# Inverse square roots of the last phase's layer norms: from a power on GpSimd to an integer estimate and Newton steps on VectorE

## Chip, cores and metric

The kernel runs on one core of a Trainium2 chip. The metric is the device time of one execution in microseconds. Activations, weights and matmuls are fp32. The engines are named PE (TensorE), DVE (VectorE), ACT (ScalarE), POOL (GpSimd) and SP (SyncE, which issues most DMAs).

## What is computed

64 graphs of 128 nodes with 128 features each ("64 tiles") go through four layers; in each, a graph network and then an expert network are added to x, both behind a layer norm:

```
def _layernorm(x, axis=-1, eps=1e-05):
    m = jnp.mean(x, axis=axis, keepdims=True)
    v = jnp.var(x, axis=axis, keepdims=True)
    return (x - m) / jnp.sqrt(v + eps)
...
x = x + _L0_gnn_ref(_layernorm(x), adj, ...)       # adjacency, PReLU
x = x + _L0_ffn_ref(_layernorm(x), ...)            # 6 experts, top 2
x = x + _L1_gnn_ref(_layernorm(x), ...)            # convolutions, attention, GRU
x = x + _L1_ffn_ref(_layernorm(x), ..., edge_index)# gates from graph attention over 524288 edges
x = x + _L2_gnn_ref(_layernorm(x), adj, ...)       # second norm inside, with gamma and beta; x + relu(conv)
x = x + _L2_ffn_ref(_layernorm(x), ...)            # one shared and 8 routed experts, top 2, gelu
x = x + _L3_gnn_ref(_layernorm(x), nodemask, adj, W) # masked softmax attention
x = x + _L3_ffn_ref(_layernorm(x), ...)            # 8 experts, top 2, relu
```

The gates of the L1 expert network are a layer norm over 16 values (4 heads by 4 experts) of each node's attention sums, averaged over the heads, and a top 2 of 4 with softmax weights. So each norm needs 1/sqrt(variance + eps): one number per node for the 128 features, and one per node for the 16 attention sums.

## The kernel before, in words

There are two phases. The **first phase** (to about 1700 us) does L0, the graph network of L1, the sorting of the edges, the two expert results of L1 (written to `results_dram`), and the attention sums and gates of the first half of the tiles (32 of 64; step `gates`). Its own layer norms take their roots from a POOL instruction (L868), one per group of four tiles. The **last phase** does the edges and gates of the second half (steps `rows`, `edge`, then `late`), the sum of L1's experts, and L2 and L3.

In the last phase the 64 tiles are 16 groups of 4 (`GT`), and two groups make a turn of 8 (`PAIR`). The steps, per turn or group, are: `sum` (L1's expert results by their gates into x), `lift` (norm of 8 tiles, added to x), `enter` (norm of 8 tiles with gamma and beta), `adj`, `xt`, `agg`, `conv` (PE: adjacency and convolution), `settle` (DVE: relu(conv) + x, norm of 4 tiles, stored to `sent` for the experts), `route`, `mark`, `list` (top 2 and slot tables), then the expert passes: SP fetches weights, `pull` (POOL, two indirect DMAs, L2025) brings the tokens of a pass, `flip` (PE transpose), `raise` and `lower` (24 matmuls of L2075), `take` (DVE, L2442 for the shared and L2446 for the routed experts). `gather` (POOL, L2040) brings the results back, `back` adds them, `ease` is L3's norm of 8 tiles, `mask`, `soften`, `pt`, `mix` its attention, `blend` (DVE) adds it and norms 4 tiles for the last expert network, whose passes run in the same way. The second half of the edges is woven in: `rows` (POOL, L79: indirect DMAs of table rows, four or more for one group of tiles), `edge` (DVE, L137 to L170), and when all are done `late` (DVE, L240 and `half_gates`, L2638 to L2657), the gates of tiles 32 to 63. The sums of those tiles, and with them `lift`, `enter` and all that follows for turns 4 to 7, need `late`; turns 0 to 3 don't.

**Order.** No engine chooses its work at run time. A planner in the program (`plan_c`, with the durations in `LONG`) simulates the steps and writes one list, `order`; each engine walks this list and executes, in its order, the pieces that are its own, waiting on semaphores. So an instruction that waits holds up all that stands behind it on its engine. The durations in the table affect the order alone.

**Norm.** `norm()` of the last phase is on DVE: statistics per tile (L2285), their aggregation (L2288), the variance plus eps into `ln_var` (L2291, 128x8 or 128x4: one column per tile), then a wait for `rstd_ready`, and the normalization per tile (L2294). The root itself is `invert` on POOL (L2013), `ln_var` to the power `minus_half`; POOL reaches it where the list has the norm, behind the DMAs that stand ahead of it, and waits there for `var_ready`. There are 56 such norms: 24 of 8 tiles (8 `lift`, 8 `enter`, 8 `ease`) and 32 of 4 (16 `settle`, 16 `blend`). The gates need two more roots of 128x32 (L890 in the first phase, L2056 in the last), between L2643 and L2645 of `half_gates`.

`link` adds an increment of the DVE's own semaphore to an instruction and waits for it before the next, so linked instructions run strictly one after the other. All buffers of the roots (`ln_var`, `ln_rstd`, `ln_mv`) exist once.

Of the kernel before, what the change touches and what calls it, by code (L numbers as in the profile page):

```python
# [12 lines left out]
P = 128  # L13
# [5 lines left out]
GT = 4  # L19
# [10 lines left out]
SLOPE = 0.2  # L30

# [172 lines left out]
def begin_half(nc, dve, env, link, L, half, last_in, logits, weights, nth):  # L204
# [26 lines left out]
    link(v.tensor_tensor(acc, acc, last_acc, ALU.add))  # L231

# [212 lines left out]
def sort_plan():  # L445
# [64 lines left out]
    "gates": [(DVE, 10.5), (POOL, 2.2), (DVE, 9.0), (ACTE, 0.3), (DVE, 17.0)], "most": [(POOL, 2.0)],  # L510
# [179 lines left out]
def phase_a(nc, env, edge_index, weights):  # L690
# [14 lines left out]
    with ExitStack() as ctx:  # L705
# [12 lines left out]
        gates_asked, gates_answered = sem("gates_var_and_diff_ready"), sem("gates_rstd_and_exp_ready")  # L718
# [122 lines left out]
        def _(pool):  # L841
# [22 lines left out]
            for what, k in order:  # L864
# [22 lines left out]
                elif what == "gates":  # L887
                    further_gathers(pool, env, O, 0)
                    pool.wait_ge(gates_asked, 1)
                    g_.tensor_tensor(G.var, G.var, env.minus_half[:, 0:HALF], ALU.pow).then_inc(gates_answered, 1)  # L890
# [286 lines left out]
        def _(act):  # L1177
# [84 lines left out]
            for what, k in order:  # L1262
# [67 lines left out]
                elif what == "gates":  # L1330
                    further_weights(nc, act, env, O, 0)
                    act.wait_ge(gates_asked, 2)
# [395 lines left out]
def batch_of(turn):  # L1728
# [4 lines left out]
    "rows": [(POOL, 7.5)], "edge": [(DVE, 3.0), (ACTE, 0.4), (DVE, 4.0)], "late": [(DVE, 7.5), (POOL, 1.2), (DVE, 9.0), (ACTE, 0.3), (DVE, 17.0)],  # L1733
    "load2": [(SP, 2.0)], "sum": [(DVE, 2.8)], "lift": [(DVE, 4.0), (POOL, 1.6), (DVE, 4.2)], "enter": [(DVE, 4.0), (POOL, 1.6), (DVE, 5.6)],
    "adj": [(PE, 0.8), (ACTE, 0.6)], "xt": [(PE, 0.8), (ACTE, 0.6)], "agg": [(PE, 1.1), (ACTE, 0.6)], "conv": [(PE, 3.0)],
    "settle": [(DVE, 2.7), (POOL, 1.1), (DVE, 1.4)], "f2_xt": [(PE, 0.8), (ACTE, 0.6)], "f2_score": [(PE, 0.9), (DVE, 0.3)],
    "route": [(DVE, 4.5), (PE, 0.5), (DVE, 6.0)], "mark": [(DVE, 2.8), (PE, 0.9)], "list": [(DVE, 0.3)], "save": [(SP, 0.5)], "pull": [(POOL, 2.6)], "gather": [(POOL, 5.2)], "gather_last": [(POOL, 5.2)],
    "load3": [(SP, 2.0)], "back": [(DVE, 5.8)], "ease": [(DVE, 4.0), (POOL, 1.6), (DVE, 2.8)],
    "g3_xt": [(PE, 0.8), (ACTE, 0.6)], "project": [(PE, 1.0), (ACTE, 0.6)], "compare": [(PE, 1.1)], "mask": [(DVE, 5.0)], "soften": [(ACTE, 2.0)],
    "pt": [(PE, 0.8), (ACTE, 0.6)], "mix": [(PE, 1.1)], "blend": [(DVE, 3.6), (POOL, 1.1), (DVE, 1.4)],  # L1740
# [116 lines left out]
def phase_c(nc, env):  # L1857
# [12 lines left out]
    with ExitStack() as ctx:  # L1870
# [44 lines left out]
        step, var_ready, rstd_ready = sem("vector_step"), sem("var_ready"), sem("rstd_ready")  # L1915
# [21 lines left out]
        late_asked, late_answered, late_gates = sem("late_var_and_diff_ready"), sem("late_rstd_and_exp_ready"), sem("late_gates_ready")  # L1937
# [69 lines left out]
        def _(pool):  # L2007
            norms = [0]

            def invert(tiles):  # L2010
                norms[0] += 1
                pool.wait_ge(var_ready, norms[0])
                nc.gpsimd.tensor_tensor(env.ln_rstd[:, 0:tiles], env.ln_var[:, 0:tiles], env.minus_half[:, 0:tiles], ALU.pow).then_inc(rstd_ready, 1)  # L2013

# [253 lines left out]
        @block.vector  # L2268
        def _(dve):
            v = nc.vector  # L2270
            count, norms = [0], [0]

            def link(ins):
                count[0] += 1
# [593 lines left out]
```

## Time and profile before

| | us |
|---|---|
| median of 3 runs | 3252.85 |
| lowest and highest of them | 3246.36, 3257.89 |
| the profiled execution, its own time | 3252.75 |
| its span | 3251.0 |
| PE busy in the span | 2330.9 (72%) |
| DVE busy | 1980.0 (61%) |
| ACT busy | 1283.0 (39%) |
| POOL busy | 1334.2 (41%) |
| mean granted clock of PE | 0.848 |

No engine is full over the whole span; the program is a chain of stages with different limits. A row of the timeline reads: start, busy time, engine, line of the program, operation, what it writes <- what it reads, and in brackets the idle time of the engine just before it with the instruction that ended it. "issue" means that the profile shows nothing that the engine waited for. POOL's busy time includes the time in which it writes the descriptors of its indirect DMAs.

### The profile page before, as it was taken

The page shows a single profiled execution, that of the slowest core. Times are in us where ns is not written, and L with a number is a line of the kernel's source. Part 1 is how long each engine was busy: PE and PEld are TensorE (multiplying, and loading weights), DVE is VectorE, ACT ScalarE, POOL GpSimd, SP SyncE. Part 2 cuts the span into 40 slices and gives each one's busy share as a digit, 9 for nine tenths or more (in the row PEclk, how much of TensorE's full clock was granted, in tenths as well). Part 3 has the DMA queues.
Part 4 walks back from the last instruction along what each step waited for, and adds up shares of the span by engine and source line. Part 5 has one row for each costly group of instructions (what it writes and reads, how often), then busy time and mean ns, then how long its engine had stood idle before and what let it go on. Part 6 is the DMA issues. An engine that isn't in the chain of part 4 may idle for free. (4 is left out here: it accounts for less than half of the span.)

```text
span 3251.0 us, 41129 instructions
## 1 busy us (share of the span) xinstructions
PE 2330.9 (72%) x12088; PEld 1724.5 (53%) x12088; DVE 1980.0 (61%) x5040; ACT 1283.0 (39%) x2786; POOL 1334.2 (41%) x1229
## 2 busy tenths in 40 slices
PE   5677777777788578888813317496878899797980
PEld 3334444444444344555513306386867888787980
DVE  7999877777785632256557765677675155755122
ACT  4234445554444344455402203242344455343540
POOL 0011100111017500067765777424522776664576
PEclk8788788888888789999956658798988999898995
DMA  3000000000021200033312125253525776665972
GB/s 122 0 24 11 21 7 14 14 14 14 14 42 42 69 14 14 30 101 81 77 45 64 45 47 135 61 157 105 144 78 128 202 191 190 151 186 142 225 213 75
DMA packets 306804, 269.01 MB, mean 83 GB/s; under 512 B 92730, under 2 KB 237100, under 8 KB 305916
## 3 DMA queue, kind: packets, MB, share of 16 engines
q1 hardware_dynamic: 271772, 220.14, 23.6%
q0 software_dynamic: 34784, 46.03, 7.1%
q8 instruction: 99, 1.62, 0.2%
q14 instruction: 149, 1.22, 0.1%
HBM read 203.57 MB, written 63.70 MB: 82 GB/s over the span
## 5 line engine op out<-in xcount | busy, mean ns | idle before, releaser
L868 POOL TENSOR_TENSOR a_rstd<-a_var,minus_half 128x4 f32<-128x4 f32 x64 | 108.8, 1701 | 1104.4 <-DVE a_var L1414 1097.3
L1512 DVE TENSOR_TENSOR room<-room 128x1024 f32<-128x1024 f32 (+1 forms) x356 | 488.2, 1392 | 55.6 <-ACT room L1260 46.8
L2025 POOL DMA_INDIRECT c_slots<-sent,c_tokens_of_slots x340 | 353.4, 1039 | 309.0 <-PE bank L2194 221.8
L2075 PE MATMUL bank<-c_expert_w,weights_f 128*128 128x128 f32 x2720 | 349.8, 287 | 41.7 <-DVE c_made L2446 20.4
L2266 ACT ACTIVATE weights_f<-bank,c_expert_b 128x256 f32<-128x256 f32 x680 | 278.5, 470 | 249.1 <-PE bank L2075 247.9
L2075 PEld LDWEIGHTS bank<-c_expert_w,weights_f 128*128 128x128 f32 x2720 | 344.2, 203 | 50.9 <-issue 38.3
L2075 PE MATMUL bank<-c_slots_t,c_expert_w 128*128 128x256 f32 x1360 | 351.9, 406 | 22.6 <-ACT weights_f L2266 19.0
L2075 PEld LDWEIGHTS bank<-c_slots_t,c_expert_w 128*128 128x128 f32 x1360 | 266.1, 206 | 60.2 <-issue 23.9
L900 PE MATMUL bank<-a_h1p,weights_a 128*128 128x512 f32 x544 | 248.5, 605 | 4.2 <-ACT a_dist_exp L1237 4.2
L2446 DVE TENSOR_TENSOR c_made<-bank,c_expert_b 128x256 f32<-128x256 f32 x170 | 72.2, 425 | 268.8 <-PE bank L2075 261.1
L79 POOL DMA_INDIRECT got_room<-table_dram,own_rows x184 | 193.5, 1052 | 66.6 <-issue 66.0
L900 PE MATMUL bank<-a_xt,weights_a 128*128 128x512 f32 (+1 forms) x352 | 193.5, 641 | 27.0 <-DVE a_conv L1455 14.0
L79 POOL DMA_INDIRECT room<-table_dram,own_rows x178 | 181.1, 1018 | 69.5 <-issue 69.5
L900 PEld LDWEIGHTS bank<-weights_f,a_h 128*128 128x128 f32 x1024 | 123.8, 196 | 89.2 <-ACT a_h L1219 67.1
L900 PEld LDWEIGHTS bank<-a_h1p,weights_a 128*128 128x128 f32 x544 | 102.1, 194 | 120.1 <-issue 113.6
L900 PE MATMUL bank<-weights_f,a_h 128*128 128x128 f32 x1024 | 133.1, 285 | 44.6 <-ACT a_h L1219 25.7
L1185 ACT ACTIVATE a_xh<-a_x,a_shift,a_rstd 128x128 f32<-128x128 f32 x256 | 104.2, 482 | 145.3 <-DVE a_shift L1419 145.3
L2040 POOL DMA_INDIRECT got_room<-made,c_places x128 | 133.7, 1045 | 52.3 <-issue 37.7
L411 PE MATMUL bank<-ident,room 128*128 128x128 f32 x192 | 35.0, 326 | 167.4 <-DVE room L2298 92.3
L2040 POOL DMA_INDIRECT room<-made,c_places x128 | 129.0, 1008 | 49.8 <-issue 39.4
L411 PE MATMUL bank<-ident,a_xh 128*128 128x128 f32 x192 | 42.1, 359 | 147.4 <-ACT a_xh L1185 147.4
L2256 ACT ACTIVATE c_slots_t<-bank 128x256 f32<-128x256 f32 x170 | 65.1, 383 | 188.9 <-PE bank L2194 188.8
(496 smaller groups left out, 4745.8 us busy)
## 6 DMA issues: line engine op xcount, KB each, us to landing
c_expert_w<-in_weights_c SPq DMA_DIRECT2D x340, 256.0 KB
made<-c_made SPq DMA_DIRECT2D x170, 128.0 KB
results_dram<-a_results SPq DMA_DIRECT2D x64, 256.0 KB
room<-results_dram SPq DMA_DIRECT2D x16, 1024.0 KB, 7.5
c_expert_b<-in_f_b SPq DMA_DIRECT2D x170, 64.0 KB
room<-in_adj SPq DMA_DIRECT2D x32, 256.0 KB, 5.5
sent<-c_rows_to_send SPq DMA_DIRECT2D x32, 256.0 KB, 2.4
c_slots<-sent,c_tokens_of_slots POOLq DMA_INDIRECT x340
```

What stands on the lines that cost most here:

```text
L79: pool.indirect_dma_start(out=dst, out_offset=None, in_=env.rows_dram, in_offset=bass.IndirectOffsetOnAxis(ap=index, axis=0), bounds_check ...
L411: ins = nc.tensor.transpose(bank[0:n, j * P:(j + 1) * P], src[:, j, 0:n], ident[:, :])
L868: rstd.did(g_.tensor_tensor(st.rstd[:, :], st.var[:, :], env.minus_half[:, 0:GT], ALU.pow), what, k)
L900: return nc.tensor.matmul(out, lhsT=lhsT, rhs=rhs, start=start, stop=stop, skip_group_check=True)
L1185: ins = go(st.XH[:, j, :], st.X[:, j, :], ACT.Identity, bias=st.shift[:, j:j + 1], scale=st.rstd[:, j:j + 1])
L1512: v.tensor_tensor((dv[:, :, 0, :], other(dv))[j], sv[:, :, 0, :], other(sv), (ALU.min, ALU.max)[j]).then_inc(sort_step, 1)
L2025: pool.indirect_dma_start(out=XS[p.r % S_BUFS][:, j, :], out_offset=None, in_=env.sent_dram[p.q], in_offset=bass.IndirectOffsetOnAxis(ap=T ...
L2040: pool.indirect_dma_start(out=rooms[turn % 2][:, c, t, :], out_offset=None, in_=env.made_dram[q], in_offset=bass.IndirectOffsetOnAxis(ap=P ...
L2075: return nc.tensor.matmul(out, lhsT=lhsT, rhs=rhs, start=start, stop=stop, skip_group_check=True)
L2256: go(XST[p.r % 2][:, :], XB[:, 0:SLOT], ACT.Copy).then_inc(flip_copied, 1)
L2266: go(H[p.m % 2][:, c, :], U[c // 2][:, (c % 2) * SLOT:(c % 2 + 1) * SLOT], func, bias=bias).then_inc(hidden, 1)
L2446: ins = v.tensor_tensor(YB[p.r % Y_BUFS][:, :, :], y, bcast(B2[p.r % W_BUFS][:, :], [P, SLOT_TILES, D], 1), ALU.add)
```

## The change

Every root of `norm()` and of `half_gates` (both halves) is now made by DVE in `inverse_root`: the bits of x shifted right by one and subtracted from a constant give an estimate, and each of three Newton steps is out = out * (1.5 - x/2 * out * out). These are 12 linked instructions in place of one wait: three for the estimate and -x/2, nine for the steps. `ln_var` is now linked too. POOL has no piece of these steps any more, and the semaphores `var_ready` and `rstd_ready` are gone; the exchange on the gates keeps only the exponential of ACT. In the gates `mean`, `top.max1` and `top.max2`, which are free there, serve as rooms. The norms of the first phase (L868) stay as they were. The planner's durations are changed to match.

```diff
@@ new function, of both phases @@
+ROOT_BITS, ROOT_STEPS = 0x5F3759DF, 3
+def inverse_root(nc, link, out, x, half, square):
+    v = nc.vector
+    bits = square.bitcast(I32)
+    link(v.tensor_scalar(bits, x.bitcast(I32), 1, None, ALU.logical_shift_right))
+    link(v.tensor_scalar(out.bitcast(I32), bits, -1.0, float(ROOT_BITS), ALU.mult, ALU.add))
+    link(v.tensor_scalar(half, x, -0.5, None, ALU.mult))
+    for step in range(ROOT_STEPS):
+        link(v.tensor_tensor(square, out, out, ALU.mult))
+        link(v.tensor_tensor(square, square, half, ALU.mult))
+        ins = v.scalar_tensor_tensor(out, square, 1.5, out, ALU.add, ALU.mult)
+        if step < ROOT_STEPS - 1:
+            link(ins)
+    return ins
 
 
...
@@ planner costs @@
-    "gates": [(DVE, 10.5), (POOL, 2.2), (DVE, 9.0), (ACTE, 0.3), (DVE, 17.0)], "most": [(POOL, 2.0)],
+    "gates": [(DVE, 22.5), (ACTE, 0.3), (DVE, 16.0)], "most": [(POOL, 2.0)],
...
-    "rows": [(POOL, 7.5)], "edge": [(DVE, 3.0), (ACTE, 0.4), (DVE, 4.0)], "late": [(DVE, 7.5), (POOL, 1.2), (DVE, 9.0), (ACTE, 0.3), (DVE, 17.0)],
-    "load2": [(SP, 2.0)], "sum": [(DVE, 2.8)], "lift": [(DVE, 4.0), (POOL, 1.6), (DVE, 4.2)], "enter": [(DVE, 4.0), (POOL, 1.6), (DVE, 5.6)],
+    "rows": [(POOL, 7.5)], "edge": [(DVE, 3.0), (ACTE, 0.4), (DVE, 4.0)], "late": [(DVE, 22.5), (ACTE, 0.3), (DVE, 16.0)],
+    "load2": [(SP, 2.0)], "sum": [(DVE, 2.8)], "lift": [(DVE, 9.8)], "enter": [(DVE, 11.3)],
...
-    "settle": [(DVE, 2.7), (POOL, 1.1), (DVE, 1.4)], "f2_xt": [(PE, 0.8), (ACTE, 0.6)], "f2_score": [(PE, 0.9), (DVE, 0.3)],
+    "settle": [(DVE, 5.7)], "f2_xt": [(PE, 0.8), (ACTE, 0.6)], "f2_score": [(PE, 0.9), (DVE, 0.3)],
...
-    "load3": [(SP, 2.0)], "back": [(DVE, 5.8)], "ease": [(DVE, 4.0), (POOL, 1.6), (DVE, 2.8)],
+    "load3": [(SP, 2.0)], "back": [(DVE, 5.8)], "ease": [(DVE, 8.5)],
...
-    "pt": [(PE, 0.8), (ACTE, 0.6)], "mix": [(PE, 1.1)], "blend": [(DVE, 3.6), (POOL, 1.1), (DVE, 1.4)],
+    "pt": [(PE, 0.8), (ACTE, 0.6)], "mix": [(PE, 1.1)], "blend": [(DVE, 6.6)],
@@ GpSimd, first phase @@
                     further_gathers(pool, env, O, 0)
-                    pool.wait_ge(gates_asked, 1)
-                    g_.tensor_tensor(G.var, G.var, env.minus_half[:, 0:HALF], ALU.pow).then_inc(gates_answered, 1)
@@ GpSimd, last phase @@
-            norms = [0]
-
-            def invert(tiles):
-                norms[0] += 1
-                pool.wait_ge(var_ready, norms[0])
-                nc.gpsimd.tensor_tensor(env.ln_rstd[:, 0:tiles], env.ln_var[:, 0:tiles], env.minus_half[:, 0:tiles], ALU.pow).then_inc(rstd_ready, 1)
-
...
                     further_gathers(pool, env, env.further_room, 1)
-                    pool.wait_ge(late_asked, 1)
-                    nc.gpsimd.tensor_tensor(G.var, G.var, env.minus_half[:, 0:HALF], ALU.pow).then_inc(late_answered, 1)
-                elif what in ("lift", "enter", "ease"):
-                    invert(PAIR)
-                elif what in ("settle", "blend"):
-                    invert(GT)
@@ VectorE, norm() @@
                 link(ins)
-                norms[0] += 1
-                v.tensor_scalar(env.ln_var[:, 0:tiles], mv[:, 0:tiles, 1], LN_EPS, None, ALU.add).then_inc(var_ready, 1)
-                dve.wait_ge(rstd_ready, norms[0])
+                link(v.tensor_scalar(env.ln_var[:, 0:tiles], mv[:, 0:tiles, 1], LN_EPS, None, ALU.add))
+                link(inverse_root(nc, link, env.ln_rstd[:, 0:tiles], env.ln_var[:, 0:tiles], env.ln_half[:, 0:tiles], env.ln_square[:, 0:tiles]))
                 for j in range(tiles):
@@ half_gates() @@
-    v.tensor_scalar(var, var, 1.0 / 16, LN_EPS, ALU.mult, ALU.add).then_inc(asked, 1)
-    dve.wait_ge(answered, 1)
+    link(v.tensor_scalar(var, var, 1.0 / 16, LN_EPS, ALU.mult, ALU.add))
+    link(inverse_root(nc, link, mean, var, top.max1, top.max2))
+    var = mean
...
-    dve.wait_ge(answered, 2)
+    dve.wait_ge(answered, 1)
```

The steps `lift` and `enter` drop their POOL piece in the table too, as does every step that had one for a norm. With other durations the planner writes another list for the last phase: `late` moves from place 263 of its list to place 228, ahead of the steps `sum`, `lift` and `enter` of the fourth turn, and the first `gather` and `back` steps move behind `lift` and `enter` of the last turn. The first phase's list is the same. DVE has 696 more instructions (58 roots by 12).

**DVE, the first norm of the last phase (`lift` of turn 0).** Before:

```order
L2288 BN_AGGR ln_mv<-ln_stats 128x2 x8
L2291 TENSOR_SCALAR ln_var<-ln_mv 128x8
L2294 TENSOR_SCALAR room<-x,ln_mv,ln_rstd 128x128 x8
L2314 TENSOR_TENSOR x<-x,room 128x1024
```

and now (the two further Newton steps repeat the rows of L244 to L246):

```order
L2293 TENSOR_SCALAR ln_var<-ln_mv 128x8
L240 TENSOR_SCALAR ln_square<-ln_var 128x8
L241 TENSOR_SCALAR ln_rstd<-ln_square 128x8
L242 TENSOR_SCALAR ln_half<-ln_var 128x8
L244 TENSOR_TENSOR ln_square<-ln_rstd 128x8
L245 TENSOR_TENSOR ln_square<-ln_square,ln_half 128x8
L246 SCALAR_TENSOR_TENSOR ln_rstd<-ln_square,ln_rstd 128x8
...
L2296 TENSOR_SCALAR room<-x,ln_mv,ln_rstd 128x128 x8
L2316 TENSOR_TENSOR x<-x,room 128x1024
```

Between `ln_var` and the normalization stand twelve small instructions where DVE waited for POOL.

**POOL, around the last edge rows (`lift`, `enter` of turn 2 and `settle` of groups 4 and 5; `c_slots` is a pull of the expert passes, `got_room` an edge row).** Before:

```order
L2025 DMA c_slots<-sent,c_tokens_of_slots 128x128 x16
L2013 TENSOR_TENSOR ln_rstd<-ln_var,minus_half 128x8
L2025 DMA c_slots<-sent,c_tokens_of_slots 128x128 x4
L2013 TENSOR_TENSOR ln_rstd<-ln_var,minus_half 128x8
L2025 DMA c_slots<-sent,c_tokens_of_slots 128x128 x4
...
L79 DMA got_room<-table_dram,own_rows 128x24 x4
...
L79 DMA got_room<-table_dram,own_rows 128x24 x2
...
L2025 DMA c_slots<-sent,c_tokens_of_slots 128x128 x2
L2013 TENSOR_TENSOR ln_rstd<-ln_var,minus_half 128x4
...
L79 DMA got_room<-table_dram,own_rows 128x24 x10
L97 UNCONDITIONAL_BRANCH
L2013 TENSOR_TENSOR ln_rstd<-ln_var,minus_half 128x8
L2025 DMA c_slots<-sent,c_tokens_of_slots 128x128 x4
```

and now:

```order
L2034 DMA c_slots<-sent,c_tokens_of_slots 128x128 x20
...
L80 DMA got_room<-table_dram,own_rows 128x24 x4
...
L80 DMA got_room<-table_dram,own_rows 128x24 x2
...
L2034 DMA c_slots<-sent,c_tokens_of_slots 128x128 x6
...
L80 DMA got_room<-table_dram,own_rows 128x24 x10
L98 UNCONDITIONAL_BRANCH
L2034 DMA c_slots<-sent,c_tokens_of_slots 128x128 x2
```

From the first row shown to the last `got_room` row POOL had four powers and 28 pull DMAs around them (16, 4, 4, 2 and 2); now there is no power, and 26 pull DMAs (20 and 6); the other 2 come behind the last row. A fifth power, that of `lift` of turn 3, stood right behind the last row.

**DVE, right behind the gates of `late`** (`got_room` holds the last operands of the gates; `c_made` and `x<-x,bank` are the `take` of a pass). Before:

```order
L2656 TENSOR_TENSOR got_room<-got_room 128x1024
L2657 TENSOR_REDUCE gates<-got_room 128x32
L2446 TENSOR_TENSOR c_made<-bank,c_expert_b_0 128x256
L2446 TENSOR_TENSOR c_made<-bank,c_expert_b_1 128x256
L2329 SCALAR_TENSOR_TENSOR x<-bank,x 128x512
L2285 BN_STATS ln_stats<-x 128x6 x4
```

and now:

```order
L2659 TENSOR_TENSOR got_room<-got_room 128x1024
L2660 TENSOR_REDUCE gates<-got_room 128x32
L2444 TENSOR_TENSOR x<-x,bank 128x256 x2
L2310 SCALAR_TENSOR_TENSOR x<-room,gates,x 128x128 x8
L2444 TENSOR_TENSOR x<-x,bank 128x256
L2448 TENSOR_TENSOR c_made<-bank,c_expert_b_3 128x256
L2310 SCALAR_TENSOR_TENSOR x<-room,gates,x 128x128 x8
L2288 BN_STATS ln_stats<-x 128x6 x8
```

The sums of turn 3 (L2310), its `lift` and `enter`, and the takes of some eight passes follow `late` now; before, they stood ahead of it.

## Rows read from the trace of the kernel before

**Rows 1.** Busy time by stretch: from:to, length, PE, PEld, DVE, ACT, POOL (instructions), granted clock, DMA share, GB/s

```profile
1866.00:2110.00 244.00, 108.92 (x666) 96.72 (x666) 152.26 (x431) 53.95 (x122) 165.56 (x149) 0.71 0.32 81
2110.00:2245.00 135.00, 110.88 (x755) 101.75 (x756) 106.01 (x361) 46.77 (x107) 31.68 (x28) 0.90 0.47 129
2245.00:2364.00 119.00, 103.48 (x699) 95.00 (x698) 76.66 (x299) 45.46 (x109) 72.21 (x66) 0.94 0.51 140
2364.00:2960.00 596.00, 511.64 (x3287) 464.11 (x3286) 322.60 (x1022) 271.69 (x679) 345.14 (x332) 0.89 0.62 164
```

**Rows 2.** DVE idle until POOL's root (us, times): stretch 1710:1866, then those of rows 1

```profile
  POOL ln_rstd L2013: 20.2, 8
...
  POOL ln_rstd L2013: 44.9, 6
...
  POOL ln_rstd L2013: 13.9, 10
...
  POOL ln_rstd L2013: 30.0, 9
...
  POOL ln_rstd L2013: 89.2, 23
```

**Rows 3.** Timeline of DVE: the first norm, and two small linked instructions of an edge

```profile
1729.11 0.17 DVE L2291 TENSOR_SCALAR ln_var<-ln_mv 128x8 f32<-128x8 f32 x1
1731.07 2.14 DVE L2294 TENSOR_SCALAR room<-x,ln_mv,ln_rstd 128x128 f32<-128x128 f32 x8 [1.79 <-POOL ln_rstd L2013]
...
1737.02 0.17 DVE L144 TENSOR_TENSOR got_room<-att_max,got_room 128x8 f32<-128x8 f32 x1
1737.22 0.17 DVE L145 TENSOR_TENSOR got_room<-att_max,got_room 128x8 f32<-128x8 f32 x1
```

**Rows 4.** Groups by form on POOL: busy us, mean ns, idle before and its releaser

```profile
L2013 POOL TENSOR_TENSOR ln_rstd<-ln_var,minus_half 128x4 f32<-128x4 f32 x32 | 33.1, 1035 | 71.4 <-DVE ln_var L2291 71.0
```

**Rows 5.** Timeline of DVE: the gates of the first half and the edges behind them

```profile
1666.74 0.69 DVE L2645 TENSOR_TENSOR room<-room 128x512 f32<-128x512 f32 x1 [5.58 <-POOL room L890]
...
1692.89 0.29 DVE L214 TENSOR_TENSOR room<-own_rows 128x128 f32<-128x128 f32 x1 [1.73 <-DMA own_rows<-table_dram,node_id]
```

**Rows 6.** Timeline of POOL: a root and the pull behind it, and the last edge row

```profile
1964.19 1.68 POOL L2013 TENSOR_TENSOR ln_rstd<-ln_var,minus_half 128x8 f32<-128x8 f32 x1
1966.05 1.07 POOL L2025 DMA_INDIRECT c_slots<-sent,c_tokens_of_slots  x1 [0.18 <-issue]
...
2047.91 1.00 POOL L79 DMA_INDIRECT got_room<-table_dram,own_rows  x1 [0.31 <-issue]
```

**Rows 7.** Timeline of DVE: lift of turn 3, the last edge, start and end of late

```profile
2050.64 2.20 DVE L2294 TENSOR_SCALAR room<-x,ln_mv,ln_rstd 128x128 f32<-128x128 f32 x8 [17.36 <-POOL ln_rstd L2013]
...
2065.82 0.35 DVE L140 TENSOR_TENSOR got_room<-got_room,own_rows 128x184 f32<-128x184 f32 x1 [0.66 <-DVE got_room L137]
...
2075.05 0.23 DVE L240 TENSOR_SCALAR att_den<-att_den 128x128 f32<-128x128 f32 x1 [2.06 <-issue]
...
2109.12 1.22 DVE L2657 TENSOR_REDUCE gates<-got_room 128x32 f32<-128x1024 f32 x1
```

**Rows 8.** Timeline of PE: first and last matmuls of turn 3's transposition, aggregation and convolution

```profile
2064.25 1.04 PE L411 MATMUL bank<-ident,room 128*128 128x128 f32 x8
...
2073.59 0.38 PE L2075 MATMUL bank<-bias_parts,bias_ones 65*128 65x512 bf16 x1
```

**Rows 9.** Timelines of DVE and PE: one norm of the long stretch and who waits

```profile
2598.55 1.68 DVE L2294 TENSOR_SCALAR room<-x,ln_mv,ln_rstd 128x128 f32<-128x128 f32 x6 [8.17 <-POOL ln_rstd L2013]
...
2600.80 1.54 PE L411 MATMUL bank<-ident,room 128*128 128x128 f32 x6 [7.72 <-DVE room L2294]
```

**Rows 10.** Tile ln_rstd, 2364 to 2960: PE's waits for the normalized tiles (us, times)

```profile
  PE bank L411: 24.0, 7
```

**Rows 11.** Timeline of POOL: a DMA issue beside L2656 of DVE, and one beside L144, L145

```profile
1678.52 1.73 POOL L861 DMA_INDIRECT own_rows<-table_dram,node_id  x1 [0.30 <-issue]
...
1736.96 1.00 POOL L79 DMA_INDIRECT got_room<-table_dram,own_rows  x1 [0.30 <-issue]
```

More of the change, by code:

```diff
@@ L717, in phase_a @@
         rows_in = [sem(f"edge_rows_in_{u}") for u in range(EDGE_ROOMS[0])]
-        gates_asked, gates_answered = sem("gates_var_and_diff_ready"), sem("gates_rstd_and_exp_ready")
+        gates_asked, gates_answered = sem("gates_diff_ready"), sem("gates_exp_ready")
         rooms_cleared, last_in, rows_used, logits, weighed = sem("rooms_cleared"), sem("last_row_loaded"), sem("edge_rows_used"), sem("logits_ready"), sem("weights_ready")
@@ L1331, in _ @@
                     further_weights(nc, act, env, O, 0)
-                    act.wait_ge(gates_asked, 2)
+                    act.wait_ge(gates_asked, 1)
                     go(G.top.diff_exp[:, :], G.top.diff[:, :], ACT.Exp).then_inc(gates_answered, 1)
@@ L1913, in phase_c @@
         WG = sb("place_weights", [P, 2 * BATCHES, 2, MOST_TILES])
-        step, var_ready, rstd_ready = sem("vector_step"), sem("var_ready"), sem("rstd_ready")
+        step = sem("vector_step")
         results_in, adj2_in, adj3_in, mask_in = ([sem(f"{n}_{s}") for s in range(STREAMS)] for n in ("results_in", "adj2_in", "adj3_in", "mask_in"))
@@ L1936, in phase_c @@
         rooms_cleared, kept_in = sem("rooms_cleared"), sem("weights_kept_loaded")
-        late_asked, late_answered, late_gates = sem("late_var_and_diff_ready"), sem("late_rstd_and_exp_ready"), sem("late_gates_ready")
+        late_asked, late_answered, late_gates = sem("late_diff_ready"), sem("late_exp_ready"), sem("late_gates_ready")
         block = ctx.enter_context(nc.Block())
@@ L2215, in _ @@
                     further_weights(nc, act, env, env.further_room, 1)
-                    act.wait_ge(late_asked, 2)
+                    act.wait_ge(late_asked, 1)
                     go(G.top.diff_exp[:, :], G.top.diff[:, :], ACT.Exp).then_inc(late_answered, 1)
@@ L2270, in _ @@
             v = nc.vector
-            count, norms = [0], [0]
+            count = [0]
             def link(ins):
@@ L2694, in program @@
         env.ln_rstd = sb("ln_rstd", [P, STREAMS * GT])
-        env.ln_var = sb("ln_var", [P, STREAMS * GT])
+        env.ln_var, env.ln_half, env.ln_square = (sb(f"ln_{n}", [P, STREAMS * GT]) for n in ("var", "half", "square"))
         env.minus_half = sb("minus_half", [P, NT])
```

## Prediction, made blind

> **What bounds the kernel now.** I read the page's busy shares first: no engine is above 72% of the span, so a sum of busy times decides nothing and the stretches have to be read one by one. The view of busy time by stretch [rows 1] shows what each is short of. From 1866 to 2110 the busiest engine is POOL (165.6 of 244 us), which issues the edge rows and the pulls; DVE waits for it. From 2110 to 2245 DVE (106 us, and 13.9 us of waits for roots) and PE (111) are both near the 135 us. From 2245 to 2364, and above all from 2364 to 2960, PE is (103 of 119, 512 of 596). Behind 2960 no norm is left that I count.
>
> Then I read the waits for the tile `ln_rstd`, in the same stretches [rows 2]: 20.2, 44.9, 13.9, 30.0 and 89.2 us, together 198.2 us in 56 waits. That is what the change attacks. A wait is 1.79 us where POOL stands idle and ready [rows 3], but 17.36 us where the power stands behind edge rows in POOL's queue [rows 7]. So it is mostly a wait for POOL's queue, not for the power. Last I looked at who waits for the normalized tile on PE, since only that reaches the end in the PE-bound stretches [rows 9, 10].
>
> **The price of the new chain.** The nearest rows are two linked operations on 128x8, of which each starts 0.20 us after the other [rows 3]. Twelve of them, and the link of `ln_var`, put the normalization some 2.45 us behind the end of `ln_var` (13 x 0.20 less the 0.17 of `ln_var` itself). The shift and the integer subtraction are on the same width, and I price them alike. Four columns are hardly cheaper than eight, since 0.17 us of so small an operation must be mostly fixed; an estimate. So each root costs DVE 2.45 us. Against an idle POOL that is 0.7 us worse for 8 tiles and, as POOL's power of 4 columns is 1.04 us rather than 1.68 [rows 4, 6], 1.3 us worse for 4 tiles. Against a loaded POOL it is better by whatever the queue took. Bounds: 12 x 0.17 = 2.0 us, and 12 x 0.25 = 3.0 us if a dependent bit operation costs half as much again in overhead.
>
> Over the whole phase 56 x 2.45 = 137 us of work replace 198 us of waits: 61 us less time of DVE. How much of it reaches the end, stretch by stretch:
>
> **Gates of the first half: −4.7 us.** The wait of 5.58 us becomes 2.45 (DVE some 3 us earlier). POOL, rid of its power of about 5.5 us, issues the rows of its own tiles earlier, so the wait of 1.73 us for them goes as well [rows 5]. Bounds −3 and −7.3 us. The stretch behind it, to 1866, has 8 roots: 8 x 2.45 = 19.6 for 20.2, −0.6.
>
> **1866 to 2110.** POOL is the bound, and loses four powers ahead of the last edge row. One of 8 columns costs the queue 1.86 us from its start to the next issue, of which 0.30 us are spent between two issues anyway [rows 6]: two of 1.56 and two of 0.93 are 5.0 us. The pull that moves behind the last rows takes away two issues, 2 x 1.3 = 2.6 us. POOL's own waits for `ln_var` between them are worth about 1 us more. With the 5 us gained before, the last edge row goes out some 14 us earlier, near 2034 instead of 2047.9 [rows 6]. The root of 17.36 us [rows 7] no longer stands between it and the last edge, so DVE can take that edge as soon as it lands (2.5 to 3 us; 2037), spends 9.2 us on it [rows 7], and starts `late` near 2046.5. `late` was 35.3 us long [rows 7] and loses 3 us as the first half did: it ends near 2079 to 2081, about 29 us earlier.
>
> That is not a gain of 29 us, because of the new order. The sums, `lift` and `enter` of turn 3 and the takes around them stood ahead of `late` and now stand behind it. From 2050.6 to the last edge that was 15.2 us of DVE [rows 7], and the sums and statistics ahead of it another 11 (estimate from its operations): 26 us. Then PE's transposition, aggregation and convolution of turn 3, which ran beside the edge and `late` for some 9.6 us [rows 8], have nothing on DVE ahead of their `settle` to hide under. 2081 + 26 + 10 = 2117 for the first `settle` behind them. Before, it came at about 2111.5, but with two expert passes less done, worth some 5 us of takes and waits: 2116.4 in the same terms. So from the gates to this point the net is about **+1 us** with the −5.3 us already in it: the earlier end of `late` is given back by what is exposed behind it. Bounds: −15 (PE's passes fill in behind `late` and half of the 29 us stays) and +8.
>
> **2110 to 2245: +8 us.** Here POOL had hardly anything to do (31.7 us) and answered at once: 10 roots cost 13.9 us. They now cost 24.5, +10.6, on an engine that has 15 us to spare in 135 [rows 1, 2]. I take three quarters on the path; bounds +3 and +10.6.
>
> **2245 to 2364: −8 us.** 9 roots, 30.0 us of waits become 22.1. PE waits for DVE's sums and norms here too; bounds 0 and −8.
>
> **2364 to 2960: −12 us.** 23 roots, 89.2 becomes 56.4, 33 us less [rows 2]. But PE is the bound, and it waited for normalized tiles in only 7 places, for 24.0 us [rows 10]. In the first of the large ones DVE's wait of 8.17 us becomes 2.45, so of PE's 7.72 us at most 5.7 can go [rows 9]; the same share of all seven is 17.8 us. Some of this PE makes up for anyway, because its next passes then find their weights and tokens ready: I take two thirds. Bounds 0 and −20.
>
> Sum: +1 + 8 − 8 − 12 = **−11 us**. The sum is made against the profiled execution, 3252.75 us, which lies on the median of the runs, 3252.85: **3242 us**.
>
> **A rule against the change.** The issues of POOL's DMAs show contention with DVE already: 1.73 us beside a two-input operation 1024 wide, 1.00 us beside the two-input operations of 8 columns [rows 11]. So narrow operations, and the chain is made of these, have not held POOL up where I can see it; the sum counts nothing for it. [...]
>
> **Rivals.**
>
> (1) *DVE becomes the bound behind `late`: slower.* The place is the stretch from 2081 to 2245, where the moved steps, 10 roots at full price and the takes are all on DVE. All 10.6 us count, and what is late there (the routing of the first batch) starts the first `gather` late, which the order now has behind the last turn's `enter` as well; if the two later stretches then give back less than 2 us of their 20, because PE runs on the late start and not on roots: 3252.75 + 1 + 10.6 = 3264.5 us. For it: DVE's 120 of 135 us. Against it: PE waits there for DVE's roots in few places. Chance 0.21.
>
> (2) *The long stretch hides it.* PE's waits for normalized tiles are replaced by waits for tokens or weights: +1 + 8 − 8 + 0, 3254 us. For it: PE busy 512 of 596 us, DMA share 0.62. Chance 0.15.
>
> (3) *POOL's freedom carries through.* The edges and pulls come early and the planner's order leaves no hole behind `late`: of the 29 us 20 stay, with −8 and −18 later and +8 between: some 3214 us, at best 3200. For it: POOL bounds the stretch from 1866, where PE has 135 us to spare. Chance 0.18.
>
> (4) *Narrow operations do hold POOL.* Nine of twelve operations of a root have two inputs: 9 x 0.17 = 1.5 us, six roots in the POOL-bound stretch, 9.2 us back of −11: 3251 us. The issue of 1.00 us [rows 11] speaks against it: chance 0.04. [...]
>
> That the change doesn't do what it says is no rival for the last phase: its order shows the powers gone. It leaves the 64 powers of the first phase, so no gain is to be looked for before 1661.
>
> **Chances.** The forecast case, −4 to −20 us, has 0.42, of which 0.30 lies beyond the 0.3% (9.8 us) that a measurement of this kernel can tell from no change, so under 3243. Faster 0.30 + 0.18 = 0.48; within 0.3%: 0.12 + 0.15 + 0.04 = 0.31; slower 0.21. The range is 3210 to 3268: it takes in rival 1 with its price on top, and leaves out the better part of rival 3 and a hole behind `late` of over 10 us more.
>
> **What would show it.** Right: chains of 12 rows with 0.20 us steps and no wait for POOL before the normalization; the last edge row near 2034 and the end of `late` near 2081; then PE with a hole of about 10 us before the convolution of turn 3; DVE's busy share from there to the routing near full; norm waits of PE in the long stretch cut to a fifth. Wrong: a `late` that ends after 2095 (POOL wasn't held by the powers), chain steps over 0.25 us, POOL issues of 1.3 us and more beside the chains (rival 4), or an unchanged PE idle sum in the long stretch (rival 2).

## The result, and the profile after

| | before | changed |
|---|---|---|
| median, us | 3247.80 | 3234.22 |
| lowest, highest | 3242.28, 3257.89 | 3226.79, 3244.11 |
| runs | 19 | 19 |
| profiled execution, span | 3252.75, 3251.0 | 3231.47, 3229.6 |
| ratio of the changed kernel to the one before | | 0.9958, 95% interval 0.9947 to 0.9968 |

The change saves 13.6 us, 0.42%. The two profiled executions lie 21.4 us apart, some 8 us more than the medians, so terms read from them carry an error of that size between them. Such scatter can lie ahead of the change: in six traces, of kernels whose work up to there is the same, the reciprocal at the head of the first half's gates starts between 1652.7 and 1659.6 us. Differences between landmarks within one trace are better than that. The landmarks show where the profiled difference arises (start of the first row of each step on DVE, us; "minus before" is changed less before):

| landmark | before | changed | minus before |
|---|---|---|---|
| first edge behind the gates of half 0 | 1692.89 | 1688.27 | −4.6 |
| settle of group 4 | 1984.98 | 1980.52 | −4.5 |
| last edge row issued (POOL) | 2047.91 | 2035.32 | −12.6 |
| last reduction of late | 2109.12 | 2077.77 | −31.4 |
| settle of group 6 | 2111.51 | 2113.82 | +2.3 |
| slot list of the second batch | 2238.83 | 2242.12 | +3.3 |
| third route | 2369.83 | 2359.33 | −10.5 |
| last route | 2965.28 | 2921.56 | −43.7 |
| end of the span | 3251.0 | 3229.6 | −21.4 |

The last two lines belong together: 43.7 us at the last route are 21.4 at the end. In the new order more passes are left behind that route. Busy time by stretch, first of the kernel before from 2960, then of the changed one from 2917, shows it (columns as in [rows 1]):

```profile
2960.00:3251.00 291.00, 184.01 (x1214) 169.74 (x1212) 74.63 (x207) 88.65 (x219) 174.96 (x174) 0.81 0.62 159
```

```profile
2917.00:3229.00 312.00, 205.43 (x1367) 190.03 (x1366) 81.23 (x228) 100.65 (x249) 194.95 (x195) 0.83 0.63 165
```

PE has 153 matmuls and 21.4 us of work more there. An early landmark is no gain by itself when the order of the work has changed. A second trace of the changed kernel (run c1_changed_again, below) has the same pattern with other sizes: −0.3 at the first edge, −2.9 at the settle of group 4, −12.9 at the last edge row, +3.7 at the settle of group 6, +5.9, −7.7 and −37.5 at the three next, and −10.7 at the end.

**The chain.** The timeline of DVE in the changed kernel, first norm behind `late` (it answers to [rows 3]):

```profile
2115.87 0.17 DVE L2293 TENSOR_SCALAR ln_var<-ln_mv 128x4 f32<-128x4 f32 x1
2116.07 0.17 DVE L240 TENSOR_SCALAR ln_square<-ln_var 128x4 int32<-128x4 int32 x1
...
2116.68 0.16 DVE L244 TENSOR_TENSOR ln_square<-ln_rstd 128x4 f32<-128x4 f32 x1
...
2118.25 0.16 DVE L246 SCALAR_TENSOR_TENSOR ln_rstd<-ln_square,ln_rstd 128x4 f32<-128x4 f32 x1
2118.45 1.11 DVE L2296 TENSOR_SCALAR c_rows_to_send<-x,ln_mv,ln_rstd 128x128 f32<-128x128 f32 x4
```

From the end of `ln_var` (2116.04) to the normalization are 2.41 us, for 4 columns; 2.45 had been priced. Over the 56 norms it is 2.41 to 2.74 us, 2.46 in the median. The integer operations take the same 0.17 us as the others, unless an issue of POOL holds them up (see rival 4).

**The edges and late.** The timeline of DVE in the changed kernel, from the last edge to the first settle (it answers to [rows 7]):

```profile
2037.46 0.35 DVE L141 TENSOR_TENSOR got_room<-got_room,own_rows 128x184 f32<-128x184 f32 x1 [26.81 <-DMA got_room<-table_dram,own_rows]
...
2046.59 0.23 DVE L258 TENSOR_SCALAR att_den<-att_den 128x128 f32<-128x128 f32 x1 [2.02 <-issue]
...
2077.77 1.22 DVE L2660 TENSOR_REDUCE gates<-got_room 128x32 f32<-128x1024 f32 x1
...
2113.82 0.69 DVE L2331 SCALAR_TENSOR_TENSOR x<-bank,x 128x512 f32<-128x512 f32 x1 [0.33 <-PE bank L2078]
```

This is the place that the experiments turn on. DVE stands idle for 26.81 us before the last edge, with the sums, `lift` and `enter` of turn 3, which need nothing of `late`, waiting behind it in the order.

PE waits in that stretch as well: its timeline has a group of matmuls that waited for a take behind `late`:

```profile
2079.71 3.75 PE L2078 MATMUL bank<-weights_kept,weights_f 128*128 128x128 f32 x16 [32.76 <-DVE x L2444]
```

**The long stretch.** Who waits on PE, waits of the changed kernel from 2353 to 2917 (us in all, times, longest); [rows 10] had 24.0 us for the normalized tiles:

```profile
PE bank L2078 <- DVE c_token_hot L2430: 31.9, 16, 2.8
...
PE bank L429 <- DVE c_rows_to_send L2296: 7.4, 6, 2.7
...
PE bank L429 <- DVE room L2296: 4.6, 2, 3.1
```

7.4 + 4.6 = 12.0 us are left of 24.0 (12.9 in the second trace).

### The profile page after: what moved, and what is told of

Same layout as the page of the kernel before. It is cut to its first block and busy times, and to the rows that moved or that the text cites. A ratio compares the mean times of both kernels' runs of the same rounds, so it can differ in the third digit from the quotient of the medians.

```text
span 3229.6 us, 41772 instructions
## 1 busy us (share of the span) xinstructions
PE 2314.7 (72%) x12088; PEld 1705.3 (53%) x12088; DVE 2097.3 (65%) x5736; ACT 1290.6 (40%) x2792; POOL 1241.5 (38%) x1171
## 5 line engine op out<-in xcount | busy, mean ns | idle before, releaser
L2078 PE MATMUL bank<-c_slots_t,c_expert_w 128*128 128x256 f32 x1360 | 338.0, 393 | 34.3 <-ACT weights_f L2269 28.9
L2078 PEld LDWEIGHTS bank<-c_slots_t,c_expert_w 128*128 128x128 f32 x1360 | 254.6, 197 | 68.6 <-issue 33.1
L80 POOL DMA_INDIRECT room<-table_dram,own_rows x178 | 182.3, 1024 | 69.5 <-issue 69.5
```

Of the source, the lines that this page charges most:

```text
L80: pool.indirect_dma_start(out=dst, out_offset=None, in_=env.rows_dram, in_offset=bass.IndirectOffsetOnAxis(ap=index, axis=0), bounds_check ...
L2078: return nc.tensor.matmul(out, lhsT=lhsT, rhs=rhs, start=start, stop=stop, skip_group_check=True)
```

## The experiments

Twelve runs were made, in four groups; the runs of a group share a chip and their runs of the kernel before. Three of the twelve repeat a kernel of the first group and one is the changed kernel again. In three groups (all but the second) the kernel before took 3553 to 3589 us (medians) instead of 3250. There the trace shows engines that start late for reasons of their own. The timeline of PE from a run of the third group, in the middle of a pass:

```profile
2215.72 0.37 PE L2075 MATMUL bank<-weights_kept,weights_f 128*128 128x128 f32 x1 [1.74 <-issue]
2217.10 0.37 PE L2075 MATMUL bank<-weights_kept,weights_f 128*128 128x128 f32 x1 [1.01 <-issue]
```

"issue" ended 141 us of PE's idle time in that run and 0.5 in the changed kernel's of the second group. On DVE, "issue" and "remote" (a release to which the profile gives no instruction) together ended 451 us against 7. Ratios of these groups are told beside the others, and no step of the sum is judged by them.

### Roots and orders apart (first group)

The edit that gives VectorE's roots the order before is the planner's table alone; the mirror image puts the new table into the kernel before:

```diff
-    "gates": [(DVE, 22.5), (ACTE, 0.3), (DVE, 16.0)], "most": ...
+    "gates": [(DVE, 10.5), (POOL, 2.2), (DVE, 9.0), (ACTE, 0.3), (DVE, 17.0)], "most": ...
-    ... "lift": [(DVE, 9.8)], "enter": [(DVE, 11.3)],
+    ... "lift": [(DVE, 4.0), (POOL, 1.6), (DVE, 4.2)], "enter": [(DVE, 4.0), (POOL, 1.6), (DVE, 5.6)],
...
```

> The changed kernel's roots on VectorE, with the planner's durations of the kernel before, so with the order before. Theory A (the new order's late gates are paid back by what then stands behind them): in the changed kernel VectorE idles 26.8 us before the last edge, because POOL's rows are late. The order before puts the sums, lift and enter of turn 3 (some 26 us) into just that hole, late starts at the same time, 2046 to 2050, and the first settle behind it comes near 2090 instead of 2113.8: 15 to 25 us less than the changed kernel, 3210 to 3220 us. Theory B (the gain came from the order, with late first): 5 to 15 us slower than the changed kernel, 3240 to 3250 us. Theory C (the order is worth nothing): 3230 to 3238 us.

Measured: 3616.11 us, ratio 1.0105 (1.0054 to 1.0156) to a kernel before of 3589.24.

> The kernel before, with powers on POOL, and the planner's durations of the changed kernel, so with the new order. Theory A (roots are what gained): the powers stand again between the edge rows, and lift of turn 3 no longer waits behind the last row; late ends some 8 to 12 us later than in the changed kernel, and the long stretch has its waits back: 3250 to 3262 us. Theory B (the order gained): 3230 to 3240 us.

Measured: 3593.37 us, ratio 1.0026 (0.9998 to 1.0054).

The number of Newton steps (1 in the first of the next two runs, 6 in the second):

```diff
-ROOT_BITS, ROOT_STEPS = 0x5F3759DF, 3
+ROOT_BITS, ROOT_STEPS = 0x5F3759DF, 1
```

> The changed kernel with one Newton step instead of three: six operations less per root, 1.2 us each, 58 roots, 70 us less work on VectorE; the order is the same. It leaves out two of the three steps, so the roots are coarse. If VectorE's chain is on the path where my sum had it (2079 to 2243: 14 roots, 17 us, three quarters; 2243 to 2353: 9 roots, 11 us, half; the seven places where PE waits later, 8 us; the gates 1.3 us): 20 to 30 us less, 3205 to 3215 us. If the passes on PE hide it: 0 to 8 us less.

Measured: 3605.60 us, ratio 1.0063 (1.0028 to 1.0097).

> The changed kernel with six Newton steps instead of three: nine operations more per root, 1.8 us each, 58 roots, 106 us more work on VectorE; the order is the same. On the path where my sum had it: 2079 to 2243 25 us and nearly all of it, 2243 to 2353 16 us and half of it, then some 12 us, the gates 2 us: 40 to 55 us more, 3275 to 3290 us. If the passes hide it: under 25 us more. If small two-input operations hold up POOL's DMA issues, issues beside the chains take over 1.3 us.

Measured: 3697.80 us, ratio 1.0327 (1.0271 to 1.0383).

Between one step and six, 15 operations per root lie, 58 x 15 = 870 in all, some 174 us at 0.20 us each; the time differs by 92 us. So in that group about half of the operations added to the chains is paid for, on the average; the 0.20 us is from the changed kernel's first trace. In absolute terms none of the four tells how roots or orders act where the kernel before takes 3250 us: the times expected were for that, and VectorE's roots in the order before lie on the other side of 1 here. This group is inconclusive for the question that it was made for.

### The same question again, and the sum's terms one by one (second group)

> The changed kernel once more, as it is, beside the others: the ground for the differences of this group. Its ratio to the kernel before was 0.996 where it was first measured; 0.993 to 0.999 expected here.

Measured: 3236.15 us, ratio 0.9939 (0.9920 to 0.9958), before 3251.53. As at first.

> Roots on VectorE with the order before, once more, beside the changed kernel. Theory A (VectorE's hole of 26.8 us before the last edge takes the sums, lift and enter of turn 3): the first settle behind late comes 15 to 25 us earlier than in the changed kernel, and the whole is 10 to 20 us below it. Theory B (the takes that stand ahead of the last edge in this order wait for PE's passes, so late starts late again): late ends 15 us or more behind the changed kernel's, and the whole is 0 to 15 us above it.

Measured: **3218.40 us, ratio 0.9897 (0.9878 to 0.9917)**, 17.8 us less than the changed kernel (four runs each, 3214.3 to 3226.1 for 3226.2 to 3242.2). Theory A holds, with its place: the whole and the first settle come as it said. Only `late` starts later than the first group's expectation had it (2057.05, not 2046 to 2050). The timeline of DVE in this run, from turn 3's normalization to the first settle:

```profile
2025.08 2.41 DVE L2296 TENSOR_SCALAR room<-x,ln_mv,ln_rstd 128x128 f32<-128x128 f32 x8
...
2057.05 0.23 DVE L258 TENSOR_SCALAR att_den<-att_den 128x128 f32<-128x128 f32 x1 [3.76 <-issue]
...
2088.26 1.22 DVE L2660 TENSOR_REDUCE gates<-got_room 128x32 f32<-128x1024 f32 x1
...
2090.61 0.69 DVE L2331 SCALAR_TENSOR_TENSOR x<-bank,x 128x512 f32<-128x512 f32 x1
```

`late` ends 10.5 us later than in the changed kernel (the last edge row goes out at 2041.86, not 2035.32), and yet the first `settle` behind it comes 23.2 us earlier (2090.61 for 2113.82): turn 3 was done in the hole. DVE's waits for the edge rows of the second half are 29.5 us up to there, and were 50.3 in the changed kernel. So the change's gain is that of the roots less a loss through the order that its durations bring about. What the same order shows against before, landmark by landmark, is the cleanest reading of the roots:

| landmark | this run | minus before | step forecast | step measured |
|---|---|---|---|---|
| settle of group 6 | 2090.61 | −20.9 | | −20.9 |
| slot list of the second batch | 2226.26 | −12.6 | +8 | +8.3 |
| third route | 2358.76 | −11.1 | −8 | +1.5 |
| last route | 2930.93 | −34.4 | −12 | −23.3 |
| end of the span | 3217.8 | −33.2 | 0 | +1.2 |

(The forecasts are the prediction's, for the stretches that end at 2245, 2364 and 2960 of before; each is set against the landmark nearest to that end.)

Next, the same kernel with the roots of ten norms given back to POOL:

```diff
+POOL_ROOTS = range(14, 24)
...
                 norms[0] += 1
+                if norms[0] - 1 in POOL_ROOTS:
+                    powers_made[0] += 1
+                    pool.wait_ge(var_ready, powers_made[0])
+                    nc.gpsimd.tensor_tensor(env.ln_rstd[:, 0:tiles], env.ln_var[:, 0:tiles], env.minus_half[:, 0:tiles], ALU.pow).then_inc(rstd_ready, 1)
```

(and on DVE the wait for `rstd_ready` for the same ten norms; order before)

> As the run before, but the ten norms behind late (numbers 14 to 23: 2110 to 2245 in the trace of before) take their roots from POOL as in the kernel before, all others from VectorE. By my sum these ten cost 24.5 us on VectorE and 13.9 us as waits, three quarters of it on the path: 8 us less than the run with all roots on VectorE. If PE has the slack there: no difference, within 3 us.

Measured: **3205.68 us, ratio 0.9858 (0.9842 to 0.9875)**, 12.7 us less than with all roots on VectorE, 42 below the kernel before. The waits are back to the size of an idle POOL's; timeline of DVE:

```profile
2085.53 0.17 DVE L2310 TENSOR_SCALAR ln_var<-ln_mv 128x4 f32<-128x4 f32 x1
2086.86 1.11 DVE L2316 TENSOR_SCALAR c_rows_to_send<-x,ln_mv,ln_rstd 128x128 f32<-128x128 f32 x4 [1.16 <-POOL ln_rstd L2032]
```

From the first settle behind `late` to the slot list of the second batch it takes 127.4 us (2083.47 to 2210.89), as before (127.3), where with all roots on VectorE it took 135.7 (2090.61 to 2226.26). So 8.2 us arise in the place where the ten norms stand. The two profiled executions are 19.0 us apart, more than the medians: 6.6 us of it stand already at the settle of group 4 (1974.43 for 1981.04), up to where the two kernels do the same, 3.1 of these at the head of the first half's gates, and 3.7 more arise behind the slot list. How much of the 12.7 is more than the 8.2 and such scatter isn't settled.

The last of the group is the kernel before, with the roots of its last 24 norms alone on VectorE:

```diff
+DVE_ROOTS = range(32, 56)
...
                 norms[0] += 1
+                if norms[0] - 1 in DVE_ROOTS:
+                    return
```

(and `inverse_root` on DVE for these; all else as in the kernel before)

> The kernel before with its order, but the last 24 norms (ease and blend, from 2350 on) take their roots from VectorE; gates and the other 32 norms stay on POOL. My sum gives the long stretch 12 us: 3236 us where before is 3248, ratio 0.996. If PE's passes hide it: no difference, within 3 us. If the long stretch is all of the gain, and more: 18 to 22 us less.

Measured: 3231.83 us, ratio 0.9931 (0.9915 to 0.9948), 19.7 us less than the kernel before. From the settle of group 4 to the third route its landmarks agree with before to 1 us (2370.01 for 2369.83 at the latter), the last route is 21.3 us earlier, the end 18.2. The waits of PE for normalized tiles in the long stretch (tile `ln_rstd`, 2364 to 2939; L430 is L411 of before), which were 24.0 us in 7 [rows 10]:

```profile
  PE bank L430: 5.7, 4
```

That is 18.3 us less of waits on PE, and 18.2 us less at the end, but the two are not the same thing. Busy time between the third and the last route, before and then in this run (columns as in [rows 1]):

```profile
2369.83:2965.28 595.45, 511.29 (x3285) 464.02 (x3285) 322.11 (x1020) 268.76 (x674) 346.86 (x333) 0.89 0.62 164
```

```profile
2370.00:2943.94 573.94, 503.03 (x3285) 456.60 (x3285) 369.12 (x1297) 268.29 (x674) 320.89 (x310) 0.90 0.65 170
```

The stretch is 21.5 us shorter. PE's idle time in it fell by 13.3 us (84.2 to 70.9), since its waits for others than these norms grew; the other 8.3 us are PE's busy time for the same 3285 matmuls, 511.3 to 503.0. Of that busy time 93.9 us ran at the lower of the two clock levels (1.2 GHz) before, and 79.2 us in this run. The run before this one and the one with all roots on VectorE show the same: 500.9 and 502.7 us of busy time, 67.6 and 69.5 of idle time. There is one trace of the kernel before; its seven runs in this group have granted clocks of 0.844 to 0.851 over the whole span, the runs of these three kernels 0.849 to 0.857. Behind the last route 3.1 us are lost again (288.9 for 285.7 us, with the same work).

### The rest (third and fourth group)

The order alone, and the six steps, are the first group's edits again.

> The kernel before, all roots on POOL, with the changed kernel's order, once more on a chip where the kernel before takes about 3250 us; it closes the square of roots and orders. The other three corners: 3251.5 (POOL, old order), 3236 (VectorE, new order), 3218 (VectorE, old order), so the new order costs 18 us with VectorE's roots. If order and roots act apart: 3251.5 + 18 = 3269 us, ratio 1.005. If the new order helps only the kernel with powers on POOL, because lift of turn 3 does not stand behind the last edge rows any more: 3240 to 3250 us.

Measured: 3569.11 us, ratio 1.0032 (1.0006 to 1.0058), before 3553.48.

> The changed kernel with six Newton steps, once more on such a chip: 1.83 us more per root, 106 us more work on VectorE in the same order. The long stretch has 24 roots, 44 us more work; where the roots were taken off POOL's queue it gained 18 to 20 us. By my sum's shares: 40 to 55 us over the changed kernel (3276 to 3291). If the passes on PE hide it: under 25 us. Expected at the landmarks: between the end of late and the second route nearly all of 12 times 1.83 us = 22 us.

Measured: 3672.49 us, ratio 1.0332 (1.0277 to 1.0386). Both repeat the first group (1.0026 and 1.0327). The new order with POOL's roots was not seen on a chip where the kernel before takes 3250 us, so whether order and roots act apart stays open; twice it came out slower than the order before, by 0.3%, the first time within its interval.

Twelve more roots on POOL, beside the ten:

```diff
-POOL_ROOTS = range(14, 24)
+POOL_ROOTS = {0, 1, 2, 4, 5, 6, 9, *range(14, 24), *range(28, 33)}
```

> The run with ten roots on POOL, and twelve more on POOL: all that waited under 2 us in the trace of before, up to number 32 (0, 1, 2, 4, 5, 6, 9 and 28 to 32). Each is 0.7 (8 tiles) to 1.3 us (4 tiles) shorter than VectorE's chain if POOL is still idle there, 11 us in all. If the wait of a root alone decides: 3 to 8 us less than the run with ten. If POOL's queue is on the path from 1866 on and VectorE has a hole there anyway: no difference, within 3 us; and if the powers now fall behind pulls that moved: 2 to 6 us more.

Measured: 3577.14 us, ratio 1.0059 (1.0034 to 1.0084), before 3553.48. There was no run with the ten alone beside it, so it says nothing of the twelve more.

And two Newton steps in place of three:

```diff
-ROOT_BITS, ROOT_STEPS = 0x5F3759DF, 3
+ROOT_BITS, ROOT_STEPS = 0x5F3759DF, 2
```

(with the ten powers on POOL and the order before)

> The run with ten roots on POOL and the order before, with two Newton steps instead of three in the 46 roots on VectorE and the two of the gates: three operations, 0.6 us, less each, 29 us less work on VectorE and 144 instructions fewer. It leaves out the last step, so the roots are good to some five millionths. On a chip where the kernel before takes about 3250 us: ratio 0.983 to 0.985 (3198 to 3203 us) if the long stretch passes on half of its 24 times 0.6 us, 0.985 to 0.987 if the passes on PE hide it. On a chip like that of the second group (before 3553 us), where instructions are late on every engine, the ratio is above 1 if what counts there is the number of instructions, and near 0.99 if it is the work.

Measured: 3604.99 us, ratio 1.0037 (1.0008 to 1.0066), before 3586.35. Of the two cases that were told apart for such a chip (3553 us, which the expectation counts to the second group, is the third's), it is the one above 1; that the number of instructions is the cause was not shown.

## Why the prediction was right, and where its steps were not

The forecast was −11 us; −13.6 was measured (3247.80 to 3234.22), and the sign was as forecast. In absolute time it was 3242 us, 7.8 too high, of which 5 are the kernel before, whose median over 19 runs is 3247.80 and not the 3252.85 of three. The steps fared less evenly than the sum, and its agreement is in part luck. Of the three steps behind `late`, +8, −8 and −12, the changed kernel's two traces show +1.0 and +2.2, −13.8 and −13.6, −10.9 and −3.0: the first two each came out some 6 us lower than forecast, and with the order before they are +8.3 and +1.5, so this is the new order's doing, which the sum didn't hold.

- **The chain, 2.45 us.** 2.41 and 2.46 us measured. Right.
- **Gates of the first half, −4.7.** −4.6 at the first edge; within one trace, from the reciprocal at the head of these gates to that edge, it is 37.5 us before and 33.0 in four traces with the new roots, so −4.5. Right, by both parts: the wait for the rows is gone from the trace. The eight roots to 1866 were priced at −0.6, and nothing can be told of them: from the first settle to the fourth it takes 88.7 us before, and 91.1 and 88.3 in the changed kernel's two traces.
- **1866 to 2110.** The last edge row was forecast near 2034 and went out at 2035.32, the start of `late` at 2046.5 and 2046.59, its end at 2079 to 2081 and 2079.0, the first settle behind it at 2117 and 2113.82. Here the argument from POOL's queue holds row by row. That from the exposed work holds in its sum, 34.8 us from the end of `late` to the settle for 36, but not in its form: the hole of about 10 us on PE ahead of turn 3's convolution isn't there. PE is busy for 31.5 of these 34.8 us, with passes that the 32.76 us of waiting had held back. What the prediction did not say is that DVE would stand idle for 26.81 us in front of the last edge, which is as long as the 26 us of moved work. The new order and the prediction's own 2034 for the last row let one expect it. The run with the order before is 17.8 us faster as a whole, and 23.2 at the settle where the trace shows the difference arise.
- **2110 to 2245, +8.** +8.3 with the order before, and 8.2 between the kernels that differ in these ten roots alone. Right: three quarters of the 10.6 us are on the path. In the changed kernel itself it is +1.0 (+2.3 to +3.3), but its order has other takes in this stretch.
- **2245 to 2364, −8.** Wrong: +1.5 with the order before, and +2.5 in the run with the ten roots on POOL. 7.9 us less of waits on DVE brought nothing, in a stretch where PE is busy for 103 of 119 us [rows 1]. The sum took DVE's waits as waits of the end; in the trace of before PE waits for these normalized tiles in one place only, for 4.6 us. The changed kernel's −13.8 there (+3.3 to −10.5) is its order's, which puts gathers and their sums behind the last turn.
- **2364 to 2960, −12, bounds 0 and −20.** Too small: −19.7 us by the time of the run that changes only these roots (ratio 0.9931), −18.2 by its profile. The first factor, 0.74 of 24.0 us, gives 17.8, and 18.3 went. The second, "I take two thirds", gives 12.2, and PE's idle time fell by 13.3: right as well. What the sum put at nothing is PE's busy time: the same 3285 matmuls took 8.3 us less, with less of them at the lower clock level; 3.1 us were lost behind the last route. In the changed kernel only 12.0 us of the 24.0 went, half and not the four fifths that its signs of being right asked for. Its −10.9 and −3.0 are mixed with the moved passes, so that one of them lies near −12 is chance.
- **Rivals.** (1) DVE as the bound behind `late`: 8.2 of the 10.6 us exist, but the later stretches give back more than they cost. (Its terms add up to 3264.35, not 3264.5.) (2) Falls with the run on the long stretch. (3) Is not what the changed kernel does, but it is what its roots do in the order before: −33.2 us in the profile, 3218 us measured where 3214 was given, by −20.9, +8.3, +1.5 and −22.1 us where the rival had −20, +8, −8 and −18. (4) Falls with the trace of the changed kernel: two-input operations of the chains fill more than half of 48 issues of POOL's DMAs, and none of these lasts over 1.01 us. One of them, timelines of POOL and of DVE:

```profile
1959.33 1.00 POOL L2034 DMA_INDIRECT c_slots<-sent,c_tokens_of_slots  x1 [0.30 <-issue]
```

```profile
1959.30 0.23 DVE L244 TENSOR_TENSOR ln_square<-ln_rstd 128x8 f32<-128x8 f32 x1
```

The issue keeps its 1.00 us and the next follows after 0.30; the operation is 0.06 us longer, the most that any two-input operation of the chains shows in this trace. Wide ones do hold an issue [rows 11], and the trace shows how: in the changed kernel 66 of 77 issues that began with 0.2 us or more of a TENSOR_TENSOR on SBUF still to run took over 1.05 us, and ended 0.87 us (median) after that operation. An operation of 0.17 us is over before that matters.

What no rival named goes the other way: issues hold the chain's one-input operations. All 13 of these that started 0.55 us or more into an issue took 0.26 to 0.42 us instead of 0.17, and ended 0.96 to 0.97 us after the issue's start; none of the others that started within an issue took over 0.20. All operations of the chains together lose 3.1 us by POOL's issues. One of them, POOL and DVE:

```profile
2299.56 0.99 POOL L2049 DMA_INDIRECT got_room<-made,c_places  x1 [0.30 <-issue]
```

```profile
2300.11 0.41 DVE L241 TENSOR_SCALAR ln_rstd<-ln_square 128x8 int32<-128x8 int32 x1
```

The Trainium skill (SBUF — State Buffer, "SBUF: two separate sides") states an exclusive lock on a port pair that the two engines share: an operation of DVE takes it in a 2-port mode, or with two SBUF inputs against a GpSimd operation that reads SBUF, and whichever starts first blocks the other to its end. The waits in both directions look like it, but not to the end of the issue, and no row shows in which mode an operation ran or when an issue reads.

## What to carry to other kernels

Moving a small result from a queue-bound engine to the one that needs it pays where the first has a queue and costs where it stands idle: the better kernel here (3206 us, ratio 0.9858) has the roots of 46 norms on DVE and leaves ten on POOL, chosen by the length of their waits in the trace. If a planner writes the order from durations, a change of durations is a second change, to be timed by itself: here it took back 17.8 us of what the roots had gained, by putting a step that waits for a transfer ahead of work that needs nothing of it. Of waits in a stretch that another engine bounds, count only those that this engine waits for itself: 7.9 us of DVE's waits were worth nothing from 2245 to 2364. Then look at that engine's busy time too: 18.3 us less of PE's waits took 13.3 us off its idle time, and another 8.3 us went with the granted clock.

## What was not expected of the hardware

The same kernel took 3248 to 3252 us where it was first measured and in the second group, and 3553 to 3589 us (medians) in the other three, with waits on "issue" and "remote" on PE, DVE and ACT where there were next to none. The ratio of two kernels did not carry over: VectorE's roots in the order before were 0.9897 (0.9878 to 0.9917) there and 1.0105 (1.0054 to 1.0156) in the first group. The record gives the first group and the second the same chip number, 12 (the third 7, the fourth 14), so the number alone doesn't tell the fast group from the slow ones. What delays the instructions was not found.
